# Graph attention on one core: a cleared buffer and a wait behind the four gathers of every chunk

## The chip, the cores and the metric

The kernel runs on one core of one Trainium2 chip. The core has a matrix engine (TensorE, PE in the profile; PEld is its weight load), VectorE (DVE), ScalarE (ACT), GpSimd (POOL) and a queue engine (SyncE, SP), which run side by side and meet through semaphores. The metric is the time of one execution on the device in microseconds; several runs are given by their median.

## What is computed

Two graph layers over 6250 nodes of 64 features and 200,000 edges sorted by receiver. The first takes segment sums over the edges. The second, in which the change lies, is attention with four heads: each edge scores its receiver's query against its sender's key, a softmax runs over the edges of a receiver, and the values are summed with these weights. Cut to its core:

```
Q, K, V = x@Wq[h], x@Wk[h], x@Wv[h]            # h = 0..3
s = (Q[:, receiver] * K[:, sender]).sum(-1) * 64**-0.5
p = exp(s - segment_max(s, receiver)[receiver])
alpha = p / segment_sum(p, receiver)[receiver]
agg = segment_sum(alpha * V[:, sender], receiver)
x = layernorm(x + (x + mean_over_heads(agg) @ Wout))
```

## The kernel before

The program has three stretches. The first (0 to about 526 us of the profile) does the sums of the first layer, its norm, and turns the normalised nodes into `U`, a table of all nodes times Wq·Wk. The last (from about 2908 us) scales the sums, applies Wv and Wout and writes the result. Between them lies the attention loop.

The attention loop goes over 391 chunks (`NCH`) of 512 edges. For each chunk the 512 rows of `x1` that belong to its senders are fetched from HBM into `XS`, a ring of 8 slots (`S2`) of four times 128 rows. GpSimd does that with four indirect DMAs, called gathers here, one for each 128 edges (L586 to L590). It issues them chunk after chunk, written out without a loop, and does nothing else in this stretch. The four gathers of chunk c add 16 each to the semaphore `xg` of their slot.

TensorE runs a software pipeline over the chunks (`attend`, L1489). In step m it turns the rows of chunk m (L1461, behind a wait for `xg`), weighs the rows of chunk m-4 with their probabilities (`weigh`, L1471, posts `pv_done`), turns the probabilities of chunk m-3 (L1466, posts `tp_done`) and scores chunk m-1 (L1513, posts `s_done`). ScalarE takes the exponentials (L1227) and copies out the turned rows and probabilities (L1193, L1237). VectorE takes the maxima (L955) and adds up sums and outputs (`update`, L883 and L886, behind a wait for `pv_done`).

A slot may be filled again when its rows have been weighed. So GpSimd waits for `pv_done` before the first gather of chunk c, until chunk c-8 is weighed, and for `s_done` before the third gather (L588). At the first chunk of every block of 8 it also waits for the block's sender numbers (`idx2_loaded`, L583). The first 8 chunks have none of these waits but the last.

The semaphores of TensorE are what all others wait for: `pv_done` is awaited by VectorE and GpSimd, `tp_done` by ScalarE.

Of the kernel before, what the change touches and what calls it, by code (L numbers as in the profile page):

```python
# [13 lines left out]
P = 128  # L14
# [8 lines left out]
def gnn_resnorm_kernel(nc, x, src, dst, edge, Wq, Wk, Wv, Wout, out):  # L23
# [48 lines left out]
    with ctx:  # L72
        def sb(name, shape, dt=F32):
            return ctx.enter_context(nc.sbuf_tensor(name, shape, dt))
# [4 lines left out]
        def sem(name):  # L79
            return ctx.enter_context(nc.semaphore(name))  # L80
# [108 lines left out]
        part1 = dst_bs[:, 2 * CH + HH + 8 * W:2 * CH + HH + 12 * W].bitcast(F32)  # L189
        assert HH + 12 * W <= CH  # L190
        ones = sb("ones", [P, 1], BF16)
        TB = 4
        GW = 4 * D
        TG = -(-NB // TB)
        TW = TB * D
        sum_e = [XS[:, k * GW:(k + 1) * GW] for k in range(2)]
# [49 lines left out]
        s_eps, s_x1, s_x1d, s_xT, s_xTc, s_up, s_uc, s_ud = (  # L246
            sem(n) for n in ("eps_set", "x1_ready", "x1_stored", "xT_done", "xT_copied", "U_done", "U_copied", "U_copied_dve"))
        turn_steps = sem("turn_steps")
        ld2 = [sem(f"dst2_loaded{k}") for k in range(SB)]
        lx2 = [sem(f"idx2_loaded{k}") for k in range(SB)]  # L250
        xg = [sem(f"x1_gathered{k}") for k in range(S2)]
# [17 lines left out]
        def xs(slot, c):  # L269
            return XS[:, (slot * CPP + c) * D:(slot * CPP + c + 1) * D]  # L270
# [22 lines left out]
        def blocks(g):  # L293
            return min(TB, NB - TB * g)

# [6 lines left out]
        def _(sp):  # L302
# [144 lines left out]
            for g in range(TG):  # L447
                sp.wait_ge(s_fin, g + 1)
                b0, nb = TB * g, blocks(g)
                full = min(nb, NB - 1 - b0)  # L450
# [7 lines left out]
        def _(pool):  # L458
# [121 lines left out]
            for c in range(NCH):  # L580
                b, k = c // S2, c % S2
                if k == 0:
                    pool.wait_ge(lx2[b % SB], 16 * (b // SB + 1) + (16 if b == NBL - 1 else 0))  # L583
                if c >= S2:
                    pool.wait_ge(pv_done, c - S2 + 5)
                for j in range(CPP):  # L586
                    if j == CPP // 2 and c >= S2:
                        pool.wait_ge(s_done, c - S2 + 6)  # L588
                    pool.indirect_dma_start(xs(k, j), None, x1_dram,  # L589
                                            bass.IndirectOffsetOnAxis(ap=idx2[b % SB][:, k * CPP + j:k * CPP + j + 1], axis=0)).then_inc(xg[k], 16)  # L590

            for g in range(TG):
                if g == 0:
# [6 lines left out]
        def _(dve):  # L600
            links = [0]

            def link(ins):

                links[0] += 1
                ins.then_inc(dch, 1)
                dve.wait_ge(dch, links[0])
# [384 lines left out]
            def centre_x1(g):  # L992
                b0, nb = TB * g, blocks(g)
                x_, s_ = x1v[:, b0:b0 + nb, :], present_w[:, b0:b0 + nb]
                link(dve.tensor_reduce(s_, x_, AX_X, ALU.add))
                dve.scalar_tensor_tensor(out=x_, in0=s_.unsqueeze(2).broadcast_to([P, nb, D]), scalar=-1.0 / D, in1=x_,
                                         op0=ALU.mult, op1=ALU.add)
# [19 lines left out]
            link(dve.tensor_scalar(l_st[:, :], l_st[:, :], 1e-30, None, ALU.max))  # L1017
            first = TB * WPB
            link(dve.reciprocal(l_st[:, 0:first], l_st[:, 0:first]))
# [566 lines left out]
```

## Time and profile before

| what | value |
|---|---|
| time, median of 3 runs | 2588.42 us (2585.8 to 2590.83) |
| span of the profiled execution | 2997.5 us |
| profiled, up to the first gather | 526 us |
| profiled, first gather to end of the attention loop | 526 to 2908 us |
| profiled, last stretch | 2908 to 2997.5 us |
| GpSimd busy in the profiled span | 63% |
| granted TensorE clock in the attention loop | 0.56 of full |

The execution that was profiled took 409 us longer than the median of the runs without a profile. No time of that execution beside its span is given, so the span stands for it. The three stretches are read from the span; the runs have only their total.

### The profile page before, as it was taken

The numbers are of one execution on the slowest core, as the hardware profiler recorded it, in microseconds if no ns is written. First come the engines' busy times: TensorE is split into PE (matmuls) and PEld (weight loads), VectorE is DVE, ScalarE is ACT, GpSimd is POOL, SyncE is SP. The second block draws the span as 40 slices with busy tenths as digits, with TensorE's granted clock in tenths as the row PEclk, the third lists the DMA queues.
The fourth block names the chain that finished last, engine by engine and source line by source line (L and its number), as shares of the span: only waits on it lengthen the run. The fifth ranks groups of instructions, "written<-read, shape, count | busy, mean of one in ns | idle before, by whom it ended". The sixth has DMA issues, their size and how long they took to land.

```text
span 2997.5 us, 65526 instructions
## 1 busy us (share of the span) xinstructions
PE 2424.3 (81%) x18960; PEld 1749.1 (58%) x18961; DVE 1716.4 (57%) x5572; ACT 1313.2 (44%) x3792; POOL 1892.7 (63%) x2370
## 2 busy tenths in 40 slices
PE   4999998477888888887878788888888877778877
PEld 3888887254655555555555555555555555555555
DVE  8999997454545454444444444454544444444447
ACT  5555553443444344443444344443444343434434
POOL 3888887464666666666566566666666555656640
PEclk9999995665555555555555555555555555655558
DMA  6887772111111111111121111211112111112101
GB/s 177 257 255 254 254 252 51 21 31 33 32 38 32 39 38 33 38 32 37 30 38 31 36 35 36 38 32 39 37 33 39 29 36 30 37 29 39 31 18 24
DMA packets 178767, 194.85 MB, mean 65 GB/s; under 512 B 98339, under 2 KB 101235, under 8 KB 176481
## 3 DMA queue, kind: packets, MB, share of 16 engines
q1 hardware_dynamic: 128294, 138.91, 16.5%
q0 software_dynamic: 50048, 51.35, 9.1%
q8 instruction: 136, 2.23, 0.3%
q14 instruction: 289, 2.37, 0.3%
HBM read 184.87 MB, written 5.25 MB: 63 GB/s over the span
## 4 chain that ended last, share of the span: by engine, by line
another core or an unknown queue 30%; DVE 29%; issue 21%; DVEq 10%; PE 7%; ACT 1%; POOL 1%; ACTq 0%; DMA 0%; POOLq 0%; SPq 0%
DVE O L886 5%; DVE rmax L955 5%; DVE nm_old L968 4%; DVE l_st L883 3%; DVEq L982 2%; DVE big L723 2%; DVE cur L971 2%; DVEq L908 2%; DVE XT L877 1%; DVE nm_st L974 1%; DVEq L746 1%; DVEq L886 1%; PE psS L1513 1%; DVEq L904 1%
## 5 line engine op out<-in xcount | busy, mean ns | idle before, releaser
L589 POOL DMA_INDIRECT XS<-x_dram,dst_bs x1564 | 1482.4, 948 | 900.6 <-issue 419.9
L883 DVE SCALAR_TENSOR_TENSOR l_st<-l_st,alpha,rsum 64x1 f32 x782 | 168.2, 215 | 925.0 <-remote 891.3
L1471 PE MATMUL psVX<-XS,PmPT 128*128 128x64 f32 x1568 | 334.4, 385 | 243.6 <-ACT PmPT L1237 243.6
L1513 PE MATMUL psS<-XT,Ubuf 96*128 96x512 f32 x522 | 505.8, 1071 | 17.5 <-issue 6.2
L1471 PEld LDWEIGHTS psVX<-XS,PmPT 128*128 128x128 f32 x1568 | 308.8, 293 | 302.5 <-ACT PmPT L1237 302.2
L1237 ACT COPY PmPT<-psT 128x512 f32<-128x512 f32 x196 | 114.7, 585 | 760.1 <-remote 727.8
L1471 PE MATMUL psM<-XS,dst_bs 128*128 128x64 f32 x1560 | 343.2, 398 | 60.6 <-ACT dst_bs L1237 49.4
L1471 PEld LDWEIGHTS psM<-XS,dst_bs 128*128 128x128 f32 x1560 | 341.6, 321 | 71.0 <-ACT dst_bs L1237 58.3
L955 DVE TENSOR_REDUCE rmax<-psS 128x1 f32<-128x512 f32 x391 | 270.2, 691 | 34.2 <-remote 12.7
L1513 PE MATMUL psS<-dst_bs,Ubuf 96*128 96x512 f32 x260 | 250.3, 1065 | 7.1 <-ACT Ubuf L1188 1.6
L1466 PE MATMUL psT<-ident,dst_bs 128*128 128x128 f32 x780 | 207.6, 419 | 37.1 <-issue 34.2
L1227 ACT ACTIVATE dst_bs<-psS,cur 128x512 f32<-128x512 f32 x195 | 134.0, 687 | 234.0 <-DVE cur L971 216.6
L1461 PEld LDWEIGHTS psVX<-ident,XS 128*128 128x128 f32 x392 | 88.3, 226 | 220.8 <-issue 220.6
L1461 PEld LDWEIGHTS psN<-ident,XS 128*128 128x128 f32 x390 | 87.2, 224 | 216.6 <-issue 216.6
L1466 PE MATMUL psT<-ident,PmPT 128*128 128x128 f32 x784 | 203.7, 413 | 11.1 <-issue 7.1
L1227 ACT ACTIVATE PmPT<-psS,cur 128x512 f32<-128x512 f32 x196 | 134.7, 687 | 176.3 <-issue 99.0
L1237 ACT COPY dst_bs<-psT 128x512 f32<-128x512 f32 x195 | 114.1, 585 | 163.5 <-remote 130.5
L877 DVE TENSOR_SCALAR XT<-big,win_ids 32x512 f32<-32x512 f32 x269 | 129.3, 481 | 76.4 <-issue 76.0
L1466 PEld LDWEIGHTS psT<-ident,PmPT 128*128 128x128 f32 x784 | 162.5, 245 | 14.6 <-issue 8.8
L1466 PEld LDWEIGHTS psT<-ident,dst_bs 128*128 128x128 f32 x780 | 138.9, 216 | 54.5 <-issue 43.5
L1513 PEld LDWEIGHTS psS<-XT,Ubuf 96*128 96x128 f32 x522 | 135.1, 318 | 60.2 <-issue 60.1
L511 POOL TENSOR_TENSOR XS<-XS,zm 128x384 f32<-128x384 f32 x98 | 148.7, 1517 | 27.6 <-DVE zm L754 26.6
(281 smaller groups left out, 4133.2 us busy)
## 6 DMA issues: line engine op xcount, KB each, us to landing
big<-in_edge_attr_2x SPq DMA_DIRECT2D x342, 256.0 KB, 3.3
big<-dst_turned SPq DMA_DIRECT2D x49, 512.0 KB
XS<-x_dram,dst_bs POOLq DMA_INDIRECT x1564
O<-in_edge_attr_2x SPq DMA_DIRECT2D x48, 256.0 KB, 3.4
O<-codes_dram SPq DMA_DIRECT2D x200, 6.0 KB
x_dram<-x SPq DMA_DIRECT2D x12, 128.0 KB, 1.9
out<-big SPq DMA_DIRECT2D x12, 128.0 KB
codes_dram<-O SPq DMA_DIRECT2D x3, 384.0 KB
```

The source lines that it names most:

```text
L511: pool.tensor_tensor(buf[:, :, W:2 * W], buf[:, :, 0:W], zm[k // 2 % 2][:, :].unsqueeze(2).broadcast_to([P, 2 * SJ, W]), ALU.mult).then_in ...
L589: pool.indirect_dma_start(xs(k, j), None, x1_dram, bass.IndirectOffsetOnAxis(ap=idx2[b % SB][:, k * CPP + j:k * CPP + j + 1], axis=0)).the ...
L877: dve.tensor_scalar(t[D:96, :], dst_b[J // S2 % SB][:, J % S2 * CH:(J % S2 + 1) * CH], ids, None, ALU.not_equal).then_inc(s, 1)
L883: dve.scalar_tensor_tensor(out=ls, in0=ls, scalar=al[half], in1=rs[half], op0=ALU.mult, op1=ALU.add)
L886: last = dve.scalar_tensor_tensor(out=o, in0=o, scalar=al[half], in1=ps[half, :], op0=ALU.mult, op1=ALU.add)
L955: dve.tensor_reduce(rmax[:, q:q + 1], psSc[q][:, :], AX_X, ALU.max)
L1227: act.activation(Pms[a][:, :], psSc[a][:, :], ACT.Exp, bias=cur[:, a:a + 1], accum_out=rsum[:, a:a + 1]).then_inc(exp_done, 1)
L1237: act.copy(PTs[a][:, :], psT[:, :]).then_inc(pt_done, 1)
L1461: last = pe.transpose(psXc[b][:, j * P:(j + 1) * P], two, ident[:, :])
L1466: last = pe.transpose(ps[:, j * P:(j + 1) * P], probs[:, j * P:(j + 1) * P], ident[:, :])
L1471: last = pe.matmul(ps, pt[:, j * P:(j + 1) * P], xs(J % S2, j), start=(j == 0), stop=(j == CPP - 1))
L1513: pe.matmul(psSc[1 - a][:, :], Ubuf[1 - a][:, :], XT[(J - 1) % 3][:, :], start=True, stop=True).then_inc(s_done, 1)
```

## The change

Behind the four gathers of each chunk GpSimd clears a buffer of 128 partitions by 256 fp32 values that nothing else uses, and waits until that clear has ended before it goes on to the next chunk. The clear posts the new semaphore `pause_over`. It is done 391 times, the first 8 chunks among them. Nothing else changes, and the rows of the other engines are the same in number and kind.

```
+        pause = sb("pause", [P, 256])
...
+        s_pause = sem("pause_over")
...
             for c in range(NCH):
                 ...
                 for j in range(CPP):
                     ...
                     pool.indirect_dma_start(xs(k, j), None, x1_dram, ...).then_inc(xg[k], 16)
+                pool.memset(pause[:, :], 0.0).then_inc(s_pause, 1)
+                pool.wait_ge(s_pause, c + 1)
```

On GpSimd, in the middle of the attention loop, the kernel before has this row of gathers (the name in front is the ring, the one in brackets the semaphore waited for):

```order
L589 DMA XS<-x1_dram,dst_bs 128x64 [waits pv_done]
L589 DMA XS<-x1_dram,dst_bs 128x64
L589 DMA XS<-x1_dram,dst_bs 128x64 [waits s_done]
L589 DMA XS<-x1_dram,dst_bs 128x64
L589 DMA XS<-x1_dram,dst_bs 128x64 [waits pv_done]
```

In the same place the changed kernel has a clear in front of each `pv_done`, and the first gather of the next chunk carries two waits:

```order
L593 MEMSET pause 128x256
L591 DMA XS<-x1_dram,dst_bs 128x64 [waits pv_done,pause_over]
L591 DMA XS<-x1_dram,dst_bs 128x64
L591 DMA XS<-x1_dram,dst_bs 128x64 [waits s_done]
L591 DMA XS<-x1_dram,dst_bs 128x64
L593 MEMSET pause 128x256
L591 DMA XS<-x1_dram,dst_bs 128x64 [waits pv_done,idx2_loaded0,pause_over]
```

No gather has changed its place against another; one clear and one wait stand between each four.

## Rows read from the trace of the kernel before

**Rows 1.** Page, part 1: busy time, share and instructions of each engine.

```profile
PE 2424.3 (81%) x18960; PEld 1749.1 (58%) x18961; DVE 1716.4 (57%) x5572; ACT 1313.2 (44%) x3792; POOL 1892.7 (63%) x2370
```

**Rows 2.** Page, part 4: the chain that ended last, by engine.

```profile
another core or an unknown queue 30%; DVE 29%; issue 21%; DVEq 10%; PE 7%; ACT 1%; POOL 1%; ACTq 0%; DMA 0%; POOLq 0%; SPq 0%
```

**Rows 3.** Windows: length, then busy time (instructions) by engine.

```profile
core 0: us, PE busy (x) PEld busy (x) DVE busy (x) ACT busy (x) POOL busy (x), PEclk, DMA share, GB/s
0.00:526.00 526.00, 442.77 (x11728) 398.20 (x11730) 492.36 (x956) 286.83 (x468) 406.35 (x793) 0.94 0.69 214
526.00:594.00 68.00, 31.58 (x146) 18.10 (x146) 26.92 (x72) 30.30 (x88) 30.68 (x33) 0.64 0.08 16
594.00:2908.00 2314.00, 1886.78 (x6270) 1283.05 (x6269) 1133.09 (x4366) 955.90 (x3116) 1451.70 (x1532) 0.56 0.18 34
2908.00:2997.50 89.50, 63.17 (x819) 49.71 (x817) 64.00 (x181) 40.22 (x123) 3.98 (x13) 0.77 0.09 21
```

**Rows 4.** The gathers' line: shortest, median and longest, in ns.

```profile
L589 POOL DMA_INDIRECT XS<-x_dram,dst_bs x1564: 938/944/1187, 526.7 to 2906.6; - x196
```

**Rows 5.** Timeline of GpSimd, two chunks: start, length, in brackets idle time before.

```profile
1541.50 0.94 POOL L589 DMA_INDIRECT XS<-x_dram,dst_bs  x1 [1.98 <-remote]
1542.74 0.94 POOL L589 DMA_INDIRECT XS<-x_dram,dst_bs  x1 [0.30 <-issue]
...
1550.23 0.94 POOL L589 DMA_INDIRECT XS<-x_dram,dst_bs  x1 [0.30 <-issue]
1553.14 0.94 POOL L589 DMA_INDIRECT XS<-x_dram,dst_bs  x1 [1.97 <-remote]
```

**Rows 6.** Timeline of PE, ACT and DVE in these two chunks.

```profile
1541.32 0.59 ACT L1237 COPY PmPT<-psT 128x512 f32<-128x512 f32 x1 [4.76 <-remote]
1541.38 0.45 DVE L883 SCALAR_TENSOR_TENSOR l_st<-l_st,alpha,rsum 64x1 f32 x2 [5.02 <-remote]
...
1541.96 1.97 PE L1471 MATMUL psVX<-XS,PmPT 128*128 128x64 f32 x8 [1.50 <-ACT PmPT L1237]
...
1547.28 1.80 PE L1471 MATMUL psM<-XS,dst_bs 128*128 128x64 f32 x8
...
1548.87 1.06 PE L1466 MATMUL psT<-ident,PmPT 128*128 128x128 f32 x4
...
1552.97 0.58 ACT L1237 COPY PmPT<-psT 128x512 f32<-128x512 f32 x1 [4.81 <-remote]
1553.02 0.45 DVE L883 SCALAR_TENSOR_TENSOR l_st<-l_st,alpha,rsum 64x1 f32 x2 [5.08 <-remote]
```

**Rows 7.** Waits, 594 to 2908 us: total, times, longest.

```profile
DVE l_st L883 <- remote: 891.3, 183, 7.9
ACT PmPT L1237 <- remote: 727.8, 151, 8.6
POOL XS L589 <- issue: 410.5, 1330, 1.7
POOL XS L589 <- remote: 361.9, 188, 2.5
```

**Rows 8.** Timeline of GpSimd at the start of the loop.

```profile
523.05 1.44 POOL L572 TENSOR_TENSOR x<-x,stat 128x256 f32<-128x256 f32 x3 [0.57 <-DVE stat L853]
526.73 1.16 POOL L589 DMA_INDIRECT XS<-x_dram,dst_bs  x1 [2.24 <-DMA x_dram<-x]
...
565.64 0.94 POOL L589 DMA_INDIRECT XS<-x_dram,dst_bs  x1 [0.30 <-issue]
593.72 1.14 POOL L589 DMA_INDIRECT XS<-x_dram,dst_bs  x1 [27.14 <-PE psVX L1471]
```

**Rows 9.** Groups by shape: GpSimd's clears of 256 columns.

```profile
L558 POOL MEMSET O<- 128x256 f32 x24 | 6.8, 312 | 9.2 <-DVE present_w L832 8.3 <-issue 0.9
L597 POOL MEMSET PmPT<- 128x256 f32 x13 | 4.0, 311 | 75.5 <-DVE O L1024 38.0 <-PE psM L1556 23.3 <-PE psN L1556 14.2
```

**Rows 10.** Timeline of GpSimd: two operations, the second waits for the first.

```profile
518.13 0.79 POOL L563 TENSOR_TENSOR XS<-XS,x 128x256 f32<-128x256 f32 x1
519.00 0.61 POOL L566 TENSOR_TENSOR XS<-XS,present_w 128x256 f32<-128x256 f32 x1
```

**Rows 11.** Timeline: a gather with two waits, and VectorE released by the same semaphore.

```profile
1510.81 0.21 DVE L883 SCALAR_TENSOR_TENSOR l_st<-l_st,alpha,rsum 64x1 f32 x1 [4.96 <-remote]
...
1511.41 0.94 POOL L589 DMA_INDIRECT XS<-x_dram,dst_bs  x1 [2.40 <-remote]
```

More of the change, by code:

```diff
@@ L191, in gnn_resnorm_kernel @@
         ones = sb("ones", [P, 1], BF16)
+        pause = sb("pause", [P, 256])
         TB = 4
@@ L248, in gnn_resnorm_kernel @@
         turn_steps = sem("turn_steps")
+        s_pause = sem("pause_over")
         ld2 = [sem(f"dst2_loaded{k}") for k in range(SB)]
@@ L590, in _ @@
                                             bass.IndirectOffsetOnAxis(ap=idx2[b % SB][:, k * CPP + j:k * CPP + j + 1], axis=0)).then_inc(xg[k], 16)
+                pool.memset(pause[:, :], 0.0).then_inc(s_pause, 1)
+                pool.wait_ge(s_pause, c + 1)
             for g in range(TG):
```

## The prediction

> **What bounds the kernel now.** The first thing to see is that two clocks disagree: the runs take 2588.4 us and the profiled span is 2997.5. So before any cost is added up it has to be settled which of the waits in the trace the runs have too.
>
> Read the busy times first [rows 1]. No engine is full: TensorE 81%, and GpSimd, the engine that the change touches, 63%. By that alone GpSimd has room. The chain that ended last seems to say the same: GpSimd is 1% of it, and the largest share, 30%, is "another core or an unknown queue" on a program with one core [rows 2]. That share is what has to be understood.
>
> Now the stretches [rows 3]. From 594 to 2908 us GpSimd runs 1532 gathers and is busy 1451.7 of 2314 us. One gather is recorded with 944 ns [rows 4], but in an uninterrupted row the next one starts 1.25 us after the last (1541.50, 1542.74, and six more to 1550.23): 0.30 us lie between them although nothing is waited for [rows 5]. So a gather costs 1.25 us of GpSimd's time, and a chunk 5.0. 1532 × 1.25 = 1915 us; of the 2314 us GpSimd truly waits 399, the rest of its idle time is the gap of 0.30 that belongs to each gather.
>
> What does it wait for? In the two chunks shown, TensorE has weighed a chunk by 1549.1 and turned the next one's probabilities by 1549.9. The engines that wait for exactly these two, VectorE and ScalarE, start at 1553.02 and 1552.97 [rows 6], and GpSimd at 1553.14 [rows 5]: three engines at once, three to four us after the work was done. GpSimd's last gather had started at 1550.23 and ended at 1551.17. The same picture comes back every 11.65 us, that is every two chunks: VectorE has 183 such waits, ScalarE 151, GpSimd 188 [rows 7]. TensorE's posts arrive late, in a bunch, and only after GpSimd has run dry. I call them held posts.
>
> Are held posts in the runs too? Take them out of the sum. Up to the first gather 526.7 us [rows 8]; 1564 gathers in one row, 1564 × 1.25 = 1955; the last stretch from the end of the last gather at 2907.5, 90 us. Sum: 2572. The runs take 2588.4, only 16 more. With the wait of 27 us at 593.72 for the first weighing kept [rows 8], it would be 2599. **The runs lie between the two.** So my reading is that the held posts belong to the profiled execution, and that in the runs GpSimd issues gathers with hardly a break for the whole loop: GpSimd is the bound, at 5.0 us a chunk. TensorE is nearly as slow: where no post is held, one weighing follows the other after 5.32 us (1541.96 to 1547.28) with hardly a gap between its records [rows 6], and the loop's mean clock is 0.56, between the levels of 1.2 and 2.4 GHz and close to the lower [rows 3]. In the runs a chunk takes at most (2588.4 - 526.7 - 90) / 391 = 5.04 us, so TensorE must have the upper level now and then there too. For the change it matters only that 5.04 leaves GpSimd 0.04 of air a chunk, whoever is the bound: the most that can be covered is the remainder of 16 us.
>
> **The change part by part.** Nothing is removed or moved; per chunk there is a clear and a wait. The sum is made on the runs' median of 2588.4, since the added time is on GpSimd, whose durations I take to be the same in the runs; on the profiled span it would be made on 2997.5, and there it falls into 399 us of waiting.
>
> Step 1, from the fourth gather to the clear. No row has a clear behind a gather. Of the gap of 0.30 behind a gather some belongs to its end and some to the start of the next. If all is start, the clear follows at once, 0.00; if all is end, 0.30 [rows 5]. A gather that waited starts 0.12 us after VectorE, which was released by the same semaphore (1541.50 against 1541.38, rows 5 and 6), while one operation of GpSimd that waits for the one before it starts 0.08 after that one's end (518.92 to 519.00) [rows 10]. So about 0.2 of the gap is the start of a gather. I take 0.15 for step 1, between that reading's 0.10 and the middle.
>
> Step 2, the clear: 0.31 us, from 37 clears of this very shape [rows 9].
>
> Step 3, from the clear's end to the next gather: not under 0.12 + 0.08 = 0.20, not over 0.08 + 0.30 = 0.38; I take 0.29.
>
> Step 4, taken off: the gap of 0.30 that was there.
>
> Sum: 0.15 + 0.31 + 0.29 - 0.30 = **0.45 us a chunk**; the ends are 0 + 0.31 + 0.20 - 0.30 = 0.21 and 0.30 + 0.31 + 0.38 - 0.30 = 0.69. What is queued behind the wait are the four gathers of the next chunk, and TensorE waits for these. The first 8 chunks are gathered by 566.6 us, and the next gather starts at 593.72 [rows 8]: their pauses are covered by the preparation of U, and 383 count. If that cover were gone it would be 8 × 0.45 = 4 us. 383 × 0.45 = 172 us. **2588.4 + 172 = 2761 us.** The lower end is 383 × 0.21 = 80, less the 16 us if they are air and not time around the span: 2652. The upper is 383 × 0.69 = 264: 2853. At 5.0 + 0.45 a chunk GpSimd is slower than TensorE's 5.32 at the low clock as well, so a clock that falls or rises changes little. The ring of 8 slots doesn't help: it lets GpSimd run ahead of TensorE, and the one that is late here is GpSimd.
>
> On step 1 a page of the Trainium skill, Perfetto Trace Analysis (section "DMA Instruction — SWDGE (GPSIMD)"), says that the record of such a gather ends when its descriptors are written, and that the GpSimd cores finish the instruction after that. By that rule the whole 0.30 could be its end, and the sum would go to the upper end, 2853. The start at 0.12 behind VectorE speaks for the smaller value, and I keep it.
>
> **The rivals.** (a) *The pause is hidden.* If the held posts are in the runs as well, GpSimd has 399 us of waiting in the loop, and 172 us fit into it: 2588, no change. For it: the trace shows the waits in every pair of chunks. Against it: then 1564 gathers plus these waits would have to fit into the 1971 us that the runs leave for the loop, and a gather would have to take about 1.0 us in the runs against 1.25 in the trace.
>
> (b) *The pause frees the posts, faster.* The posts come only when GpSimd has stopped issuing. If they are held in the runs too and a break behind four gathers lets them through, what goes is up to the 361.9 us that GpSimd waits for them [rows 7], against the 172 added: 2588 - 190 = 2398. It decides from the point where more than 0.9 us are freed per two chunks. Against it: GpSimd's natural stop at 1551.17 has to last about 1.8 us until the release at 1553, and the pause leaves only some 0.75 without a gather at work.
>
> (c) *The wait is dearer.* The first gather of a chunk now has two waits. Where a gather has two in the trace, at the block's first chunk, it starts 0.60 us after VectorE, not 0.12 [rows 11]. If that is so in each chunk, 0.48 more: 383 × 0.93 = 356, 2945 us. Against it: there the second wait was for what came late; here the late one should be the clear.
>
> (d) *Going over from gather to clear and back costs code loading.* The only such change in the trace is the first gather behind the norm's multiplies: 2.24 us idle, all of it put down to the store that the gather waits for [rows 8]. So a change costs 0 to 2.2 us there, and at the worst 383 × 2.2 = 843 us, 3430. A page of the skill, GPSIMD Engine Reference (section "Instruction dispatch"), gives about 6 us for the first call of freshly loaded code; by it, if each of the 383 pauses paid that, the time would be near 4900. The trace shows no stop of that length at such a place.
>
> That the wait does nothing beyond the order of the queue is the lower part of the forecast: the clear alone costs 0.31 a chunk, 2707 us.
>
> **How the numbers follow.** Forecast 70%, with 2652 to 2853 as its range; (c) 12%; (a) 10%; (b) 5%; (d) 3%. The range holds the forecast and (c), 2652 to 2945, together 82%. A difference of under 0.2%, 5 us, can't be told from none in this kernel. Slower: forecast, (c) and (d), 85%. Same: (a), 10%. Faster: (b), 5%.
>
> **What would show it.** In the profile of the changed kernel: 391 clears of 0.31 us; from the fourth gather's end to the next gather's start 0.75 us where nothing else is waited for, 1.03 to 1.23 if (c) holds, over 2 if (d); the gather itself still 0.94 and 1.25 apart within a chunk. If the held posts come from the profiled execution, its span moves much less than the runs' time, since the pauses fall into GpSimd's waits: 2990 to 3080, and those 361.9 us shrink. If the runs move by under 5 us while the clears are there, GpSimd was not the bound, and the reading of the two clocks was wrong. If they get faster, it is (b), and VectorE's 891.3 us of waiting must have fallen in the profile as well.

## The result

| kernel | median | runs |
|---|---|---|
| before | 2589.62 us | 2585.8 to 2592.46, 4 runs |
| changed | 2699.53 us | 2697.41 to 2701.04, 4 runs |

The ratio is 1.0428, with an interval of 1.0415 to 1.044: the change costs 110 us, 4.3%. The direction, the bound and the mechanism were as predicted; the size was not: 172 us had been forecast (2761 us), with a range from 2652.

The span of the changed kernel's profiled execution is 2699.3 us, and that is its time: the same execution took 2701.04. So here, other than in the profile before, span and run agree. The page's parts 1 and 4 of the changed kernel, to be read against [rows 1] and [rows 2]:

```profile
PE 2202.8 (82%) x18960; PEld 1605.3 (59%) x18961; DVE 1735.2 (64%) x5572; ACT 1314.6 (49%) x3792; POOL 2029.3 (75%) x2761
...
POOL 53%; issue 23%; PE 9%; DVE 8%; DVEq 4%; DMA 2%; ACT 1%; POOLq 0%; ACTq 0%; SPq 0%
POOL XS L591 48%; POOL pause L593 4%; DVE big L727 2%; PE psS L1517 2%; DMA XS<-x_dram,dst_bs 1%; DVEq L750 1%; PE psVX L1475 1%; PE psM L1475 1%; DVEq L773 1%; PE psT L1470 1%; DVE big L289 1%; DVE PmPT L753 1%; PE psA L1411 1%; PE psS L1411 1%; PE psA L1485 1%
```

The chain that ended last now names GpSimd: 53%, of which 48 are the gathers and 4 the clears, where [rows 2] had 1% for it and 30% for an unknown queue. That difference is not the change's work: the kernel before, profiled again below, has 46% for GpSimd as well. GpSimd's busy share is still only 75%. In the loop, nearly all the rest of its time is the gap in front of each gather, which the page counts as idle.

Two chunk borders on GpSimd in the changed kernel (start, length, idle before and who ended it), as [rows 5]:

```profile
1502.52 0.94 POOL L591 DMA_INDIRECT XS<-x_dram,dst_bs  x1 [0.30 <-issue]
1503.46 0.33 POOL L593 MEMSET pause<- 128x256 f32 x1
1504.06 0.95 POOL L591 DMA_INDIRECT XS<-x_dram,dst_bs  x1 [0.27 <-POOL pause L593]
...
1507.85 0.94 POOL L591 DMA_INDIRECT XS<-x_dram,dst_bs  x1 [0.31 <-issue]
1508.80 0.33 POOL L593 MEMSET pause<- 128x256 f32 x1
1509.39 0.95 POOL L591 DMA_INDIRECT XS<-x_dram,dst_bs  x1 [0.27 <-POOL pause L593]
```

The clear starts in the moment in which the fourth gather's record ends (1502.52 + 0.94), takes 0.33, and the next gather starts 0.27 after it. The other chunk borders show the same distances, 0.00 and 0.27. From the fourth gather's start to the next one's it is 1.54 us, where 1.25 stood before: 0.29 to 0.30 a chunk. 391 times that is 113 to 117 us.

The waits of that line and of the clear's line, for the whole execution, answer to [rows 4] and [rows 7]:

```profile
L591 POOL DMA_INDIRECT XS<-x_dram,dst_bs x1564: 940/945/1198, 529.9 to 2615.7; - x196
its engine sat idle before it (us, times) until:
  issue: 354.6, 1162
  POOL pause L593: 104.0, 384
  PE psS L1517: 6.9, 7
...
L593 POOL MEMSET pause<- x391: 325/329/602, 534.8 to 2616.6; 128x256 f32 x196
```

GpSimd waits 104.0 us for the clears' ends and 6.9 us for TensorE's scores, 5.1 of them in one place (chunk 31); the 361.9 us of "remote" [rows 7] are gone altogether. TensorE waits for gathers that have not landed, 156.9 us and 156.1 us before its turnings of rows. In the kernel before, profiled again, it does so for 147.6 and 141.2 us: there too it is TensorE that waits for GpSimd.

### The profile page after: what moved, and what is told of

Read it like the earlier page. It is cut to its first block, busy times and chain, and to the rows that moved or that the text cites. A ratio compares the mean times of both kernels' runs of the same rounds, so it can differ in the third digit from the quotient of the medians.

```text
span 2699.3 us, 66253 instructions
## 1 busy us (share of the span) xinstructions
PE 2202.8 (82%) x18960; PEld 1605.3 (59%) x18961; DVE 1735.2 (64%) x5572; ACT 1314.6 (49%) x3792; POOL 2029.3 (75%) x2761
## 4 chain that ended last, share of the span: by engine, by line
POOL 53%; issue 23%; PE 9%; DVE 8%; DVEq 4%; DMA 2%; ACT 1%; POOLq 0%; ACTq 0%; SPq 0%
POOL XS L591 48%; POOL pause L593 4%; DVE big L727 2%; PE psS L1517 2%; DMA XS<-x_dram,dst_bs 1%; DVEq L750 1%; PE psVX L1475 1%; PE psM L1475 1%; DVEq L773 1%; PE psT L1470 1%; DVE big L289 1%; DVE PmPT L753 1%; PE psA L1411 1%; PE psS L1411 1%; PE psA L1485 1%
## 5 line engine op out<-in xcount | busy, mean ns | idle before, releaser
L1517 PE MATMUL psS<-XT,Ubuf 96*128 96x512 f32 x522 | 442.9, 947 | 12.4 <-ACT Ubuf L1192 12.1
L1475 PE MATMUL psVX<-XS,PmPT 128*128 128x64 f32 x1568 | 310.2, 369 | 0.7 <-ACT PmPT L1241 0.7
L1475 PEld LDWEIGHTS psM<-XS,dst_bs 128*128 128x128 f32 x1560 | 306.8, 291 | 2.0 <-ACT dst_bs L1241 1.5
L1475 PE MATMUL psM<-XS,dst_bs 128*128 128x64 f32 x1560 | 305.4, 366 | 0.7 <-ACT dst_bs L1241 0.7
L1465 PEld LDWEIGHTS psVX<-ident,XS 128*128 128x128 f32 x392 | 58.1, 190 | 409.9 <-issue 409.3
L1465 PEld LDWEIGHTS psN<-ident,XS 128*128 128x128 f32 x390 | 58.0, 190 | 403.2 <-issue 402.9
L1465 PE MATMUL psVX<-ident,XS 128*128 128x128 f32 x392 | 115.2, 392 | 159.8 <-DMA XS<-x_dram,dst_bs 156.9
L1465 PE MATMUL psN<-ident,XS 128*128 128x128 f32 x390 | 114.1, 390 | 157.4 <-DMA XS<-x_dram,dst_bs 156.1
L1517 PE MATMUL psS<-dst_bs,Ubuf 96*128 96x512 f32 x260 | 225.7, 967 | 6.1 <-ACT Ubuf L1192 6.0
L1470 PE MATMUL psT<-ident,dst_bs 128*128 128x128 f32 x780 | 184.0, 383 | 3.0 <-ACT dst_bs L1231 2.8
```

Of the source, the lines that this page charges most:

```text
L1465: last = pe.transpose(psXc[b][:, j * P:(j + 1) * P], two, ident[:, :])
L1470: last = pe.transpose(ps[:, j * P:(j + 1) * P], probs[:, j * P:(j + 1) * P], ident[:, :])
L1475: last = pe.matmul(ps, pt[:, j * P:(j + 1) * P], xs(J % S2, j), start=(j == 0), stop=(j == CPP - 1))
L1517: pe.matmul(psSc[1 - a][:, :], Ubuf[1 - a][:, :], XT[(J - 1) % 3][:, :], start=True, stop=True).then_inc(s_done, 1)
```

## The experiments

The theory: in the runs GpSimd is the bound of the attention loop, at 1.25 us a gather; whatever is added to it there is paid in full; and the held posts of the first profile belong to that execution. Rivals: TensorE, at its low clock, is the bound beside it; the cost is the wait's and not the clear's; the held posts are in the runs, and the pause frees them.

### The kernel before, profiled again

No edit.

> The kernel before, unchanged, to see whether the late posts of TensorE (three engines released at once, three to four us after the work) are in the runs. Theory one (they belong to one profiled execution, the runs have none): time 2590 within 5 us; if the posts are held in every profiled execution the span is again near 2990 while the time stays at 2590; if not in every one, the span comes out near 2588 with GpSimd waiting under 30 us in all beyond the gap of 0.30 behind each gather. Theory two (the held posts are in the runs too, and the gathers are faster there than in the profile): where span and time agree, the gathers must stand closer than 1.25 us, near 1.0.

Measured: 2589.03 us (2585.95 to 2591.44, 10 runs), ratio to before 0.9997 (0.9988 to 1.0007), and a span of 2587.3 us for a run of 2589.06. The same parts of the page, the same view of the gathers' line, and GpSimd at its one long wait:

```profile
PE 2104.4 (81%) x18960; PEld 1548.2 (60%) x18961; DVE 1724.6 (67%) x5572; ACT 1312.9 (51%) x3792; POOL 1903.3 (74%) x2370
...
POOL 46%; issue 24%; PE 12%; DVE 9%; DVEq 4%; DMA 4%; ACT 1%; ACTq 0%; POOLq 0%; SPq 0%
...
L589 POOL DMA_INDIRECT XS<-x_dram,dst_bs x1564: 938/944/1198, 528.5 to 2503.5; - x196
its engine sat idle before it (us, times) until:
  issue: 463.0, 1519
  PE psS L1513: 12.1, 18
  PE psVX L1471: 6.4, 21
...
L589 POOL DMA_INDIRECT XS<-x_dram,dst_bs x1564 | 1493.0, 955 | 485.2 <-issue 463.0 <-PE psS L1513 12.1 <-PE psVX L1471 6.4
...
693.84 0.94 POOL L589 DMA_INDIRECT XS<-x_dram,dst_bs  x1 [6.88 <-PE psS L1513]
```

From the first gather's start to the last one's it is 1975 us, where [rows 4] had 2380, and 1563 × 1.249 = 1952 is the row of gathers without any wait. Of the 23 us between the two, only 6.6 are a wait: the one at 693.84, 6.88 with the gap of 0.30 that is always there. In the other places where TensorE is named the gap is the usual 0.30. Some 16 us are gathers with a longer record: the median is 944 ns as in the first profile, the mean is 955, where the first profile had 948; about a hundred took over 1.0 us. Why was not tried.

That is theory one: the kernel in the runs issues gathers with hardly a break. The spans of the runs say the same. For 31 executions of this kernel beside the first profiled one the span is on record, here and in the comparisons below, and all lie between 2582.8 and 2591.7 us. None leaves room for 400 us of late posts.

### The clear stays, its end is awaited a chunk later

```
                 for j in range(CPP):
                     ...
-                pool.memset(pause[:, :], 0.0).then_inc(s_pause, 1)
-                pool.wait_ge(s_pause, c + 1)
+                if c > 0:
+                    pool.wait_ge(s_pause, c)
+                pool.memset(pause[:, :], 0.0).then_inc(s_pause, 1)
```

> The clear of 256 columns stays, but its end is awaited only behind the next chunk's four gathers, where it is long over; so no gather stands behind a wait for a clear. Theory one (the clear alone costs, since GpSimd is the bound and works in order; the gap of 0.30 in front of a gather is the gather's own start): 391 x (0.33 + 0.27 - 0.30) = 117 us, as with the wait, 2695 to 2705. Theory two (the wait costs the way back to the sequencer, about 0.1 to 0.2 us a chunk): 2620 to 2665. Theory three (the wait is all, the clear hides beside the gather): 2590.

Measured: 2662.17 us (2657.47 to 2662.72), ratio 1.0283 (1.0266 to 1.03), 73 us over before. GpSimd at a chunk border in this kernel:

```profile
1502.06 0.94 POOL L591 DMA_INDIRECT XS<-x_dram,dst_bs  x1 [0.30 <-issue]
1503.00 0.33 POOL L595 MEMSET pause<- 128x256 f32 x1
1503.49 0.95 POOL L591 DMA_INDIRECT XS<-x_dram,dst_bs  x1 [0.17 <-issue]
```

The time is in the range of theory two, at its upper end. The gather now starts 0.17 behind the clear, not 0.27. The clear costs 0.33 + 0.17 - 0.30 = 0.20 us a chunk, and the wait for its end 0.10 more. Two thirds of the change's cost are the clear, one third the wait: 73 of 110 us. A wait still stands in this kernel, for a clear that is long over; whether it costs anything is not shown, since no kernel has the clear without any wait. Where the 0.10 arises is not shown either.

### A clear of 4 columns

```
-        pause = sb("pause", [P, 256])
+        pause = sb("pause", [P, 4])
```

> The clear has 4 columns in place of 256, the wait for its end stays. Short clears took 0.10 to 0.12 us in the trace of before. If each us of GpSimd is exposed and the gap before the next gather stays 0.27: 391 x (0.10 + 0.27 - 0.30) = 27 us, 2610 to 2620. If the cost is that of one more instruction and a wait, whatever its size, it stays near 2690.

Measured: 2620.69 us (2617.95 to 2623.12), ratio 1.0118 (1.0101 to 1.0135), 31 us over before. The clear's row and the next gather's:

```profile
1502.88 0.12 POOL L593 MEMSET pause<- 128x4 f32 x1
1503.27 1.02 POOL L591 DMA_INDIRECT XS<-x_dram,dst_bs  x1 [0.27 <-POOL pause L593]
```

391 × (0.12 + 0.27 - 0.30) = 35. The size of the clear is paid as it stands in the row, 0.21 us less for 252 columns less; 391 × 0.21 = 82 against 79 measured between this kernel and the changed one.

### Three gathers per chunk

```
-                for j in range(CPP):
+                for j in range(CPP - 1):
...
-                    gathers, further = CPP * (J // S2 + 1), CPP * U2 // S2
+                    gathers, further = (CPP - 1) * (J // S2 + 1), (CPP - 1) * U2 // S2
```

> The kernel before with three gathers per chunk: the fourth is left out, so a quarter of the sender rows is stale and the output isn't the reference's. TensorE, ScalarE and VectorE do all their work. If GpSimd is the bound of the loop (1.25 us a gather, 5.0 a chunk), up to 489 us go, until TensorE is the bound: between 2100 and 2500. If TensorE at its low clock is the bound (5.3 us a chunk in the trace), the time stays within 1% of 2590.

Measured: 2181.25 us (2177.7 to 2183.68), ratio 0.8423 (0.8408 to 0.8439). 408 us go with 391 gathers, where their full price would be 391 × 1.25 = 489. So GpSimd is the bound of the kernel before and TensorE is not, though its busy records in the first profile's loop summed to as much as the gathers. With a quarter of the gathers gone the bound begins to change hands. The chain that ended last in this kernel, and its gathers' line:

```profile
PE 32%; issue 20%; DVE 19%; POOL 9%; DVEq 6%; ACT 6%; DMA 6%; ACTq 1%; POOLq 0%; SPq 0%
...
L589 POOL DMA_INDIRECT XS<-x_dram,dst_bs x1173 | 1144.2, 975 | 421.5 <-issue 320.3 <-PE psS L1513 61.7 <-PE psVX L1471 21.2
```

GpSimd waits for TensorE in 59 places, 62 us beyond the usual gap, and its gathers' mean is 975 ns, which makes another 37 us. Together, against 23 us in the kernel before, that is most of the 81 us that did not go. The windows of the loop in this kernel and, below it, in the kernel before as profiled again (length, busy time by engine, mean granted clock):

```profile
526.00:2088.00 1562.00, 1270.98 (x6412) 892.08 (x6411) 1164.27 (x4428) 984.10 (x3200) 1143.09 (x1172) 0.85 0.22 43
```

```profile
526.00:2497.00 1971.00, 1597.98 (x6425) 1098.47 (x6424) 1168.16 (x4434) 985.81 (x3202) 1487.48 (x1560) 0.66 0.21 41
```

The same TensorE work took 1598 us of records at a mean clock of 0.66 and 1271 at 0.85. Its records are shorter where the gathers come faster.

### The pause behind every second chunk

```
-                pool.memset(pause[:, :], 0.0).then_inc(s_pause, 1)
-                pool.wait_ge(s_pause, c + 1)
+                if c % 2 == 1:
+                    pool.memset(pause[:, :], 0.0).then_inc(s_pause, 1)
+                    pool.wait_ge(s_pause, c // 2 + 1)
```

> The clear and its wait stand behind every second chunk only, 195 in place of 391. If each pause is exposed at its own price of 0.33 + 0.27 - 0.30 = 0.30 us, the time is 2589 + 195 x 0.30 = 2647. If the cost were one of a rhythm (a break every chunk that TensorE feels), two chunks' slack could take it up: 2590 to 2610.

Measured: 2639.83 us (2636.04 to 2642.33), ratio 1.0199 (1.018 to 1.0217). 195 pauses cost 51.6 us against before as measured with it (2588.27), 0.26 each; 391 cost 110, 0.28 each. Each pause is paid, and the ring's slack takes up none in a rhythm of two chunks. It is 7 us less than 195 × 0.30: in this profile the one wait is 3.9 us long and no longer 6.9, and the gathers' mean is 953 ns and no longer 955, 3 us less from each of the two.

### Three gathers and the pause

The edit of the run with three gathers, and the change's two lines.

> Three gathers per chunk and the clear with its wait behind them, to set beside the run with three gathers alone (2181 us; the fourth gather is left out again, so the output isn't the reference's). There GpSimd's own work sums to 528.5 + 1173 x 1.25 + 90 = 2085, so 94 us of the span are waits of GpSimd for others. If a pause costs only where GpSimd has no such waits, most of the 117 us falls into them: 2200 to 2245. If a pause costs 0.30 wherever it stands, also where GpSimd waits for others: 2291 to 2298.

Measured: 2263.82 us (2259.43 to 2269.23), 82.6 us over three gathers alone. Neither number was met. The spans of the gathers' rows (first start to last start) are 1562 and 1651 us; without waits they would be 1172 × 1.25 = 1465 for the first and 114 more for the second. So what is beyond the work fell from 97 to 72 us. Not all of that is waiting. The waits themselves, beyond the usual gap, are 62 us in 59 places without the pause and 48 us in 43 places with it: about 14 us of the pauses fell into them. Another 23 us less are the gathers' own length: their mean is 975 ns without the pause and 956 with it. Against that the clears are longer here, 356 ns in the mean where 330 were reckoned, some 10 us in all. The sum of GpSimd's own work in the expectation (2085 us) had taken all of the remainder for waits. The long waits stand in few places (one of 9.4 us without the pause, 9.2 with it), and a pause elsewhere is paid all the same.

### Two clears, each awaited

```
-                pool.memset(pause[:, :], 0.0).then_inc(s_pause, 1)
-                pool.wait_ge(s_pause, c + 1)
+                for n in range(2):
+                    pool.memset(pause[:, :], 0.0).then_inc(s_pause, 1)
+                    pool.wait_ge(s_pause, 2 * c + 1 + n)
```

> Two clears behind each chunk, each awaited before the next step. If a wait costs only what lies between an operation's end and the start of the next on GpSimd (0.08 us between two ordinary operations in the trace of before), the second costs 0.08 + 0.33 = 0.41 us: 2699 + 391 x 0.41 = 2860. If the wait between two clears costs nothing, 2828. If a wait costs a way back of 0.27 in front of any operation, 2934.

Measured: 2913.7 us (2911.04 to 2916.14), ratio 1.1257 (1.1239 to 1.1276): 214 us over the changed kernel, between the numbers. The rows:

```profile
1500.82 0.71 POOL L594 MEMSET pause<- 128x256 f32 x2
1501.91 0.95 POOL L591 DMA_INDIRECT XS<-x_dram,dst_bs  x1 [0.39 <-POOL pause L594]
...
825.53 0.94 POOL L591 DMA_INDIRECT XS<-x_dram,dst_bs  x1 [1.66 <-issue]
```

The two clears with the wait between them take 0.71, 0.38 more than one, near the 0.41 expected. But the gather starts 0.39 behind the second and no longer 0.27. The second clear and its wait cost 0.50 us in these rows (391 × 0.50 = 196) and 0.55 by the times. The other 18 us are explained by the last row: in 17 places, 22 chunks apart, the second gather of a chunk starts some 1.6 us behind the first one's end instead of 0.30, 22 us more in all, and nothing that the profile shows is waited for. The profiles of the runs above have no such stop. What it is, is open. Why the gather's start moved was not tried; in [rows 11] a gather with two waits had also started late, and there the cause was as little to be seen.

### The kernel before, profiled a third time

> The kernel before once more, one look. The held posts stood in the first profiled execution (span 2997.5) and not in the second (2587.3). If they come with a share of the profiled executions and not with the kernel, a third shows either one or the other, with nothing in between: a span near 2588 or near 2990.

Measured: 2590.81 us with a span of 2589.0 us. So of three profiles of this kernel one has the held posts and two have not, with nothing in between; and of the 32 spans on record 2997.5 us is the only one above 2592. None of the seven kernels with another GpSimd program has them in its one profile, the one with three gathers and no break included.

## Why the prediction was right in kind and too high in size

**Which clock to believe: right.** The sum of 526.7 + 1955 + 90 = 2572 us, with GpSimd issuing gathers without a break, was set against 2588.4. Profiled again, the kernel shows just that: gathers from 528.5 to 2503.5 us, and hardly a wait between them. What the prediction called air, at most 16 us, is mostly something else: of the 23 us beyond the bare row of gathers 6.6 are a wait and some 16 gathers with a longer record, while the last stretch is 84 us (2503.5 to 2587.3) and not 90. The air covered next to nothing: the changed kernel still has the one wait, 5.1 us long instead of 6.9.

**The bound: right.** Taking gathers away takes time away (408 us for a quarter of them), adding to GpSimd adds time in proportion. Rival (a), the hidden pause, and rival (b), the pause that frees the posts, would have needed held posts in the runs; none of the spans on record has room for them.

**Step 1, from the fourth gather to the clear: the term that was mis-sized.** 0.15 us was taken; the row shows 0.00. None of the gap of 0.30 stands behind a gather when a clear follows. (In front of a gather that follows an unawaited clear stand 0.17, so the gap between two gathers is more than what either side shows by itself; what the other 0.13 are is open. Sure is the distance between the gathers' starts, 1.54 us against 1.25; how it is shared out among the steps rests on where the records begin and end.) The reasoning had its sign right (a gather's start takes long), but then moved the value towards the middle of the bounds. 391 × 0.15 = 59 us, nearly all of the miss of 61. The Trainium skill's page Perfetto Trace Analysis (section "DMA Instruction — SWDGE (GPSIMD)") has the cores finish such an instruction behind its record's end. These rows neither show nor refute that. What they show is that the clear's record begins 0.00 behind the gather's, so the upper end of 2853, for which the whole 0.30 had to lie there, did not come.

**Step 2, the clear:** 0.31 taken, 0.33 measured (median; the mean is 0.34). **Step 3, clear to gather:** 0.29 taken, 0.27 measured. **Step 4:** 0.30, as taken. Sum 0.30 us a chunk and not 0.45.

**The number of pauses: wrong, small.** 383 were counted because the first 8 were thought covered by a wait for TensorE at chunk 8. That wait of 27.14 us [rows 8] stands only in the profile with the held posts. In the kernel before, profiled again, the first gather of the ninth chunk starts at 568.90 with the usual gap of 0.30. In the changed kernel the gather behind the eighth clear starts at 572.68, 0.27 after the clear, like all others. All 391 count: 391 × 0.295 = 115 us, of which 110 were measured. The 5 us that are missing, and a few more since the clears' mean is above their median, are on the other side of the balance: the gathers' mean is 951 ns in the changed kernel against 955, 6 us in all, and the one wait is 2 us shorter.

**Rival (c), two waits:** it did not come: the first gather of a chunk starts 0.27 after the clear. **Rival (d), code loading:** it did not come: gather and clear follow each other with no stop. By the 6 us that the Trainium skill's page GPSIMD Engine Reference (section "Instruction dispatch") gives for the first call of freshly loaded code, each pause would have been twenty times as long as it is; no row of the changed kernel shows a stop of that kind at a pause.

**What would show it: one point wrong.** The span was expected at 2990 to 3080 us, the held posts staying and the pauses falling into their waits. It is 2699.3, without held posts. Had only the two first profiles been compared, the changed kernel would have looked 298 us faster than the one before. It would have looked as if the pause had freed the posts, and nothing here shows that it does: the kernel before has profiles without them, unchanged.

**Open:** what held TensorE's posts in that one execution, and whether a pause prevents it. One span in 32 of the kernel before, against none in the four of the changed kernel, tells nothing on that; and the kernel with three gathers has none without any pause. Open too is why some gathers have a longer record than 944 ns, and more so in one kernel than in another.

No version meant to beat the kernel before was tried. GpSimd's time in the loop is 1564 gathers of 1.25 us, each of which takes one index per partition; one would need fewer of them that still fetch every row.

## What to carry to other kernels

An engine with a busy share of 63% or 74% can be the bound: look at the distance between the starts of its instructions, not at their lengths, and multiply by their number. When the span of a profile and the median of the runs disagree, first sum the suspected bound's work against the runs; if it fills them, waits that the profile shows on top belong to that execution, and a second profile of the same kernel settles it. A remainder over a sum of medians is not yet waiting: look first whether the mean of the long row's instructions lies above their median (955 against 944 ns here, times 1564). A gap of which no row shows the two halves should be taken at the side for which a row speaks, and not at the middle.

## What the runs showed of the hardware that was not expected

TensorE's mean granted clock in the loop goes with how densely it is fed, in kernels with the same work for it. Besides the two windows above: 0.61 in the changed kernel (526 to 2617 us) and 0.57 with two clears (526 to 2832 us):

```profile
526.00:2617.00 2091.00, 1698.80 (x6443) 1156.96 (x6443) 1184.13 (x4455) 992.03 (x3220) 1619.93 (x1958) 0.61 0.20 39
```

```profile
526.00:2832.00 2306.00, 1801.29 (x6445) 1225.02 (x6446) 1196.31 (x4452) 989.85 (x3217) 1756.44 (x2349) 0.57 0.16 35
```

With a chunk every 4.0 us it has 0.85 of full speed, every 5.0 us 0.66, every 5.3 us 0.61 and every 5.9 us 0.57; the means lie between the two levels of 2.4 GHz (1.0) and 1.2 GHz (0.5). TensorE's instructions are the same in all four; what differs is GpSimd's program (and, with three gathers, the count that TensorE waits for and rows that are stale). So the pace of the gathers is the likely cause of the clock; nothing else was varied to test that. TensorE's busy time grows when it has less to do per us, and its busy share stays near 80% in all four (81, 81, 81 and 78%). So here a busy share of 80% did not say that TensorE bounds: with two clears it has that share while GpSimd sets the pace.
